# Token numbers spread by ScalarE and the first expert's rows turned on TensorE, in a two-layer mixture-of-experts kernel

## The reference

```python
y = einsum('bct,bcd->bdt', x, L0_cond_weights[itok])        # each block times a 128x128 matrix picked by index
probs = softmax(y.reshape(4096, 1024) @ gate_w.T)           # 64 experts
w, sel = top_k(probs, 8); w = w / w.sum(-1)
# each expert takes its first 256 tokens (capacity), in token order
h = silu(rows @ wg[e]) * (rows @ wu[e])                     # 256x1024 by 1024x384, twice
out = h @ wd[e]                                             # 256x384 by 384x1024
x = x + (sum over a token's experts of w * out)
```

## Time and profile before

| | |
|---|---|
| median of 3 runs | 2473.59 us (2473.21 to 2474.43) |
| profiled execution, its own time | 2452.17 us |
| its span | 2450.4 us |
| TensorE busy (of the span) | 2386.2 us, 97% |
| DVE / ACT / POOL busy | 70% / 52% / 58% |
| granted TensorE clock, mean | 0.989 |
| mean HBM traffic over the span | 239 GB/s |

### The profile page before, as it was taken

One profiled execution on the slowest core, in us unless ns is written; L12 is line 12 of the kernel. 1 busy time (PEld: TensorE's weight loads), 2 busy tenths in 40 slices (PEclk: granted clock), 3 DMA queues, 4 the chain that ended last, 5 costly groups with the idle time before them and its releaser, 6 DMA issues.

```text
span 2450.4 us, 35529 instructions
## 1 busy us (share of the span) xinstructions
PE 2386.2 (97%) x13055; PEld 2107.1 (86%) x13055; DVE 1718.6 (70%) x2993; ACT 1271.8 (52%) x1779; POOL 1422.6 (58%) x1044
## 2 busy tenths in 40 slices
PE   8977999999999999999999999999999999999998
PEld 6755888888888888888888888888879999999998
DVE  4666887878888787888878788887852255555553
ACT  4544666666666666666666666666651211111110
POOL 4017887777777777777777777777610122222221
PEclk9988999999999999999999999999999999999999
DMA  9977998888999889898998989898874444444441
GB/s 335 347 264 259 288 284 280 281 275 279 285 285 284 279 278 279 275 282 273 284 282 277 280 275 280 272 286 282 272 200 97 95 125 127 129 127 127 127 118 53
DMA packets 248799, 583.69 MB, mean 238 GB/s; under 512 B 82793, under 2 KB 105322, under 8 KB 248498
## 3 DMA queue, kind: packets, MB, share of 16 engines
q1 hardware_dynamic: 181426, 402.26, 49.7%
q0 software_dynamic: 55808, 160.28, 24.7%
q10 hardware_dynamic: 11392, 18.88, 2.1%
HBM read 460.97 MB, written 124.53 MB: 239 GB/s over the span
## 4 chain that ended last, share of the span: by engine, by line
PE 90%; DVE 2%; DMA 1%; ACT 0%; POOL 0%; issue 0%; DVEq 0%; POOLq 0%; ACTq 0%
PE ps L656 25%; PE ps L674 21%; PE ps L776 17%; PE ps L655 13%; PE ps L727 5%; PE ps L652 4%; PE ps L760 2%; PE ps L653 2%; PE ps L741 1%; POOL Xg L489 0%; PE ps L634 0%; DMA G<-tabd,rowi 0%; DVE g L1404 0%; DMA x<-in_L_ffn_base_w 0%; PE ps L749 0%
## 5 line engine op out<-in xcount | busy, mean ns | idle before, releaser
L656 PE MATMUL ps<-XX,HR 128*128 128x512 f32 x2688 | 959.2, 396 | 0.0
L489 POOL DMA_INDIRECT Xg<-yd,idx x512 | 694.9, 1357 | 162.8 <-issue 155.4
L655 PE MATMUL ps<-XX,LR 128*128 128x256 f32 x2688 | 750.1, 279 | 0.0
L1169 DVE TENSOR_TENSOR LR<-raw,HR 128x1536 fp32r<-128x1536 f32 x384 | 656.8, 1750 | 1.6 <-ACT HR L857 1.4
L656 PEld LDWEIGHTS ps<-XX,HR 128*128 128x128 f32 x2688 | 505.2, 188 | 104.2
L857 ACT ACTIVATE HR<-raw 128x1536 fp32r<-128x1536 f32 x384 | 555.1, 1477 | 3.3 <-DMA raw<-in_L_ffn_wd 1.8
L655 PEld LDWEIGHTS ps<-XX,LR 128*128 128x128 f32 x2688 | 507.5, 189 | 17.5
L511 POOL DMA_INDIRECT accd<-ot,toki x128 | 251.0, 1961 | 170.5 <-ACT ot L889 148.8
L674 PE MATMUL ps<-LR,hH 128*128 128x512 f32 x768 | 302.5, 394 | 0.0
L674 PE MATMUL ps<-HR,hL 128*128 128x512 f32 x768 | 301.0, 392 | 0.0
L674 PE MATMUL ps<-HR,hH 128*128 128x512 f32 x768 | 298.8, 389 | 1.4 <-DVE hL L1206 1.4
(11 more groups left out here) (171 smaller groups left out, 3487.3 us busy)
## 6 DMA issues: line engine op xcount, KB each, us to landing
raw<-in_L_ffn_wg SPq DMA_DIRECT2D x128, 768.0 KB, 8.0
raw<-in_L_ffn_wu SPq DMA_DIRECT2D x128, 768.0 KB, 6.8
raw<-in_L_ffn_wd SPq DMA_DIRECT2D x128, 768.0 KB, 4.5
xt<-in_x SPq DMA_DIRECT2D x32, 512.0 KB, 7.0
yd<-yrow ACTq DMA_DIRECT2D x32, 512.0 KB, 6.3
x<-accd SPq DMA_DIRECT2D x32, 512.0 KB, 4.7
out<-osb SPq DMA_DIRECT2D x32, 512.0 KB, 3.0
accd<-xt SPq DMA_DIRECT2D x24, 512.0 KB, 6.4
```

Source lines behind the costliest of these rows:

```text
L489: eng.indirect_dma_start(Xg[:, c, q, :], None, yd4, bass.IndirectOffsetOnAxis(ap=idx4[:, e % 4, i:i + 1], axis=0))\
L655: eng.matmul(bank(out, 0, CAP), wl, xx[:, 0:CAP], start=False, stop=False)
L656: mm = eng.matmul(bank(out), wh, xx, start=False, stop=(k == 7))
L1169: eng.tensor_tensor(LR[:, (n + 2) % NHL, :], raw[:, n % NRAW, :], HR[:, (n + 2) % NHL, :].bitcast(F32), ALU.subtract).then_inc(s_L, 1)
```

## The change

The eight-column spreading of the token numbers moves from DVE and TensorE to ACT: `tokq`, `qm`, `rep`, `repeat` and the semaphore `s_fl` go, `spread(e)` comes, and `index(e)` reads `tq` from SBUF. `spread` runs for experts 1 to 63. Expert 0 gets its rows by two indirect loads of whole 4 KB rows (`gather_rows`), TensorE turns them by 16 transposes into banks 4 to 7 (`turn_0`), ACT and DVE split them from there (`high_0`, `low_0`). The order of its channels is then another one, so the first four weight units are loaded in the matching order, by eight DMAs each. SP holds unit 4 and all behind it until both row gathers have landed. DVE takes `split("uB", 0)` before the second count, ACT issues a first Silu ahead of the rows. The semaphore values shift by one expert.

```diff
@@ SP, load_unit(n) @@
-                eng.dma_start(unit_dst(n), unit_src(n)).then_inc(d_raw[n % NRAW], 16)
+                if n < NRAW:
+                    k = units[n][0]
+                    v = (wg if k[0] == "g" else wu)[0].rearrange("(f a h j) i -> j h a f i", f=4, a=32, h=2)
+                    f0 = 0 if k[1] == "A" else 2
+                    d = raw[:, n, :].rearrange("p (f h i) -> p h f i", f=2, h=2)
+                    for j in range(4):
+                        for h in range(2):
+                            eng.dma_start(d[32 * j:32 * j + 32, h], v[j, h, :, f0:f0 + 2]).then_inc(d_raw[n], 16)
+                else:
+                    eng.dma_start(unit_dst(n), unit_src(n)).then_inc(d_raw[n % NRAW], 16)
...
+                if n == NRAW:
+                    eng.wait_ge(d_xg[0], 16)
+                    eng.wait_ge(d_xg[1], 16)
                 load_unit(n)
@@ POOL @@
-            eng.memset(rep[:, :], 0.0)
-            v = rep[:, :].rearrange("p (f t) -> p f t", f=4)
-            for q in range(4):
-                ch.link(eng.affine_select(out=v, in_=v, compare_op=ALU.not_equal, fill=1.0,
-                                          base=-32 * q, pattern=[[0, 4], [-1, 32]], channel_multiplier=1))
...
+            def gather_rows():
+                eng.wait_ge(d_wy, 16 * NB // 4)
+                for s in range(NY):
+                    eng.wait_ge(d_ys[s], 16 * len(range(s, NB, NY)))
+                for s in range(NS):
+                    eng.wait_ge(d_as[s], 16 * (NB // 4))
+                eng.wait_ge(s_tok, 2)
+                for c in range(2):
+                    eng.indirect_dma_start(Xg[:, c, :, :].rearrange("p q s -> p (q s)"), None, yd,
+                                           bass.IndirectOffsetOnAxis(ap=toki[:, c * E:c * E + 1], axis=0))\
+                       .then_inc(d_xg[c], 16)
...
             def gather_x(e):
+                eng.wait_ge(s_i4, e)
                 for c in range(2):
+                    if e >= 2:
+                        eng.wait_ge(s_vt, 2 * (e - 2) + c + 1)
+                    else:
+                        eng.wait_ge(s_x0, 2 * c + 2)
...
-            gather_x(0)
+            gather_rows()
@@ PE @@
-            def repeat(e):
...
-                eng.matmul(bank(4 + e % 2, 0, 8), rep[:, :], tokq[:, e % 4, :], start=True, stop=True)\
-                   .then_inc(s_f, 1)
+            def turn_0():
+                eng.wait_ge(s_cte, NB)
+                for c in range(2):
+                    v = Xg[:, c, :, :].rearrange("p q s -> p (q s)")
+                    eng.wait_ge(d_xg[c], 16)
+                    for k in range(8):
+                        mm = eng.transpose(bank(4 + 2 * c + k // 4, (k % 4) * P, (k % 4 + 1) * P), v[:, k * P:(k + 1) * P], ident[:, :])
+                        if k % 4 == 3:
+                            mm.then_inc(s_x0, 1)
...
-                        if g == 0 and b == 0 and 0 < e < E - 2:
-                            repeat(e + 2)
                     mm.then_inc(s_up, 1)
-                    if e == 0 and b == 1:
-                        repeat(2)
...
             def down(e):
-                eng.wait_ge(s_fl, min(e + 3, E))
...
-            repeat(0)
-            repeat(1)
+            turn_0()
@@ ACT @@
+            def spread(e):
+                eng.wait_ge(s_tok, 2 * e + 2)
+                if e >= 5:
+                    eng.wait_ge(s_i4, e - 4)
+                for q in range(4):
+                    eng.activation(tq[0:32, e % 4, q, :], tokf[32 * q:32 * q + 32, e % 4, :], ACT.Copy)\
+                       .then_inc(s_tq, 1)
+                eng.wait_ge(s_tq, 4 * e)
+                for f in range(1, 4):
+                    eng.activation(tq[32 * f:32 * f + 32, e % 4, :, :], tq[0:32, e % 4, :, :], ACT.Copy)\
+                       .then_inc(s_f, 1)
+
+            def high_0(n):
+                eng.wait_ge(s_x0, n + 1)
+                c, g = divmod(n, 2)
+                eng.activation(XX[:, 0, 4 * g:4 * g + 4, c * P:(c + 1) * P],
+                               bank(4 + n).rearrange("p (j t) -> p j t", j=4), ACT.Copy).then_inc(s_h0, 1)
...
             for k in ("gA", "uA", "gB", "uB"):
                 split(k, 0)
-            for c in range(2):
-                high_x(0, c)
+            eng.activation(sil[:, 0:1], pf[:, 0:1], ACT.Silu)
+            for n in range(4):
+                high_0(n)
+            spread(1)
             split("dA", 0)
             for e in range(E):
+                if 1 <= e < E - 2:
+                    spread(e + 2)
                 if e >= 1:
                     for o in range(4):
                         result(e - 1, o // 2, o % 2)
...
                 copy_2(3 * e + 1)
+                if e == 0:
+                    spread(2)
                 silu(3 * e + 1)
@@ DVE @@
-                eng.memset(qm[32 * q:32 * q + 32, q, :], 1.0)
...
+            def low_0(n):
+                eng.wait_ge(s_h0, n + 1)
+                c, g = divmod(n, 2)
+                lo, hi = CAP + c * P, c * P
+                mm = eng.tensor_tensor(XX[:, 0, 4 * g:4 * g + 4, lo:lo + P],
+                                       bank(4 + n).rearrange("p (j t) -> p j t", j=4),
+                                       XX[:, 0, 4 * g:4 * g + 4, hi:hi + P].bitcast(F32), ALU.subtract)
+                if g == 1:
+                    mm.then_inc(s_vl, 1)
...
             def index(e):
-                eng.wait_ge(s_f, e + 1)
-                eng.tensor_scalar(idx4[:, e % 4, :], bank(4 + e % 2, 0, 8), 4.0, f4[:, 0:1], ALU.mult, ALU.add)\
-                   .then_inc(s_i4, 1)
-                eng.wait_ge(s_i4, e + 1)
-                eng.engine_nop().then_inc(s_fl, 1)
+                eng.wait_ge(s_f, 3 * e)
+                eng.tensor_scalar(idx4[:, e % 4, :], tq[:, e % 4, :, :].rearrange("p q c -> p (q c)"), 4.0, f4[:, 0:1],
+                                  ALU.mult, ALU.add).then_inc(s_i4, 1)
...
             split("uA", 0)
             count(0)
             token(0)
-            index(0)
             split("gB", 0)
+            split("uB", 0)
             count(1)
             token(1)
+            for n in range(4):
+                low_0(n)
             index(1)
-            split("uB", 0)
-            for c in range(2):
-                turn_x(0, c)
-                low_x(0, c)
             split("dA", 0)
```

More of the change, by code:

```diff
@@ L93, in adaln_ffn_kernel @@
         f4 = sb("f4", [P, 1], F32)
-        rep = sb("rep", [P, P], F32)
-        qm = sb("qm", [P, 4, 2], F32)
         laR = sb("laR", [P, 8, NA, R], F32)
@@ L110, in adaln_ffn_kernel @@
         tokf = sb("tokf", [P, 4, 2], F32, moe)
-        tokq = sb("tokq", [P, 4, 8], F32, moe)
+        tq = sb("tq", [P, 4, 4, 2], F32, moe)
         idx4 = sb("idx4", [P, 4, 8], I32, moe)
@@ L221, in adaln_ffn_kernel @@
         s_H, s_L, s_up, s_dn = sem("s_H"), sem("s_L"), sem("s_up"), sem("s_dn")
-        s_f, s_fl, s_c2, s_gs = sem("s_f"), sem("s_fl"), sem("s_c2"), sem("s_gs")
+        s_tq, s_f, s_c2, s_gs = sem("s_tq"), sem("s_f"), sem("s_c2"), sem("s_gs")
         s_hh, s_hl = sem("s_hh"), sem("s_hl")
+        s_x0, s_h0 = sem("s_x0"), sem("s_h0")
         s_sl, s_hp, s_out, s_tok, s_wc = sem("s_sl"), sem("s_hp"), sem("s_out"), sem("s_tok"), sem("s_wc")
@@ L474, in gather_tab @@
                        .then_inc(d_g[e % 2], 16)
-            def gather_x(e):
-                eng.wait_ge(s_i4, e + 1)
-                if e == 0:
-                    eng.wait_ge(d_wy, 16 * NB // 4)
-                    for s in range(NY):
-                        eng.wait_ge(d_ys[s], 16 * len(range(s, NB, NY)))
-                    for s in range(NS):
-                        eng.wait_ge(d_as[s], 16 * (NB // 4))
+            def gather_rows():
[9 more added lines that the diff above has]
+                       .then_inc(d_xg[c], 16)
+            def gather_x(e):
+                eng.wait_ge(s_i4, e)
                 for c in range(2):
-                    if e:
-                        eng.wait_ge(s_vt, 2 * (e - 1) + c + 1)
+                    if e >= 2:
+                        eng.wait_ge(s_vt, 2 * (e - 2) + c + 1)
+                    else:
+                        eng.wait_ge(s_x0, 2 * c + 2)
                     for q in range(4):
@@ L853, in split @@
                 n = pos[(k, e)]
-                eng.wait_ge(d_raw[n % NRAW], 16 * (n // NRAW + 1))
+                eng.wait_ge(d_raw[n % NRAW], 16 * (n // NRAW + 8))
                 if n >= NHL:
@@ L857, in split @@
                 eng.activation(HR[:, (n + 2) % NHL, :], raw[:, n % NRAW, :], ACT.Copy).then_inc(s_H, 1)
+            def spread(e):
[14 more added lines that the diff above has]
+                               bank(4 + n).rearrange("p (j t) -> p j t", j=4), ACT.Copy).then_inc(s_h0, 1)
             def high_x(e, c):
-                eng.wait_ge(s_vt, 2 * e + c + 1)
+                eng.wait_ge(s_vt, 2 * (e - 1) + c + 1)
                 if e >= 2:
@@ L1052, in _ @@
             eng.memset(tacc[:, :, :], 0.0)
```

(15 more changed lines are left out.)

8 lines of the change are left out of this document (removed).

## The result

The changed kernel takes **2450.44 us** (median of 4 runs, 2445.88 to 2451.52), the kernel before 2473.84 (4 runs, 2473.21 to 2474.43): ratio 0.9902, 95% interval 0.9885 to 0.9919. That is 23.4 us less; forecast were 24.5 less, 2449.1 us and a range of 2445 to 2457. The time, the range and the direction hold. The terms behind them do not all hold: one is exact, two are wrong by several microseconds in opposite directions.

A forecast was written before the change was run, and what follows sets the result against it. TensorE, carrying 90% of the chain of waits, was taken to bound the kernel. Gains of 13.8 + 9.4 + 1.6 - 0.3 = 24.5 us, taken from the median 2473.59, gave 2449.1 us, range 2445 to 2457.

The forecast's parts named there:

- Term 1: Experts' steady stage: `repeat` leaves TensorE, the period falls from 25.247 to 25.02 us, 61 x 0.227 = 13.8 us gained.
- Rivals E and F: E: memory sets the pace, 2462.9 us, chance 0.04. F: `spread` late each time, only first stage gains, same time, 0.02.
- D: Steady stage: GpSimd becomes the pace, a period of 25.6 us, 2486 us in all; chance 0.03.
- (a): Before expert 0: with weight loads held, the second table gather lands at 176.1 instead of 179.2, 3.1 us gained.
- rival B: Table and row gathers stay as slow as before: up to 5.9 us less gain, about 2453 to 2455; chance 0.12.
- (b), (c): (b) Way to the first row gather 1.0 us shorter, issue at 177.7; (c) two gathers replace eight, landing at 184.2.
- (d): Expert 0's 16 transposes on TensorE: eight take 2.1 us at clock 1.00, 4.2 at 0.50; all done at 189.2.
- (e): Last quarter of expert 0's rows copied and subtracted; `up(0)` starts at 190.6 in place of 199.96, 9.4 us gained.
- (g): Expert 0's first `up` group: TensorE arrives awake after the transposes, so 1.6 us lost at half speed is won.
- rival A: Transposes leave the clock low: second eight at half speed (+2.1), 1.6 us not won, 2452.8 us; chance 0.17.
- Term 3: Rest of expert 0: the wait before L674 becomes about 3.2 us and silu runs 0.6 later; 0.3 us lost net.
- rival C: Held loads and fills meet the gather of expert 1's rows, lengthening the hL wait: 2449 to 2454 us; chance 0.13.

The follow-up runs named there:

- `pair_back`: The changed kernel with a matmul pair of the removed shape, result unused, and its wait put back into `up(e)`: 2447.65 us, ratio 0.9966.
- `no_hold`: The changed kernel without the hold, so unit 4 and those behind it load without waiting for both row gathers: 2440.09 us, ratio 0.9931.
- `wake`: The changed kernel with 30 matmuls, results unused, on TensorE ahead of the transposes of expert 0's rows: 2446.48 us, ratio 0.9885.
- `before_again`: The kernel before, unchanged, run again for a second profile: 2457.7 us.
- `after_again`: The changed kernel, unchanged, run again on another chip: 2434.04 us against 2456.19 for the kernel before, ratio 0.9908.
- `wake_turns`: The changed kernel with 36 transposes of the identity on TensorE ahead of the transposes of expert 0's rows: 2447.47 us, ratio 0.9902.
- `late_count`: The changed kernel with `count(3)` and `token(3)` on DVE moved behind the splits uA and gB of expert 1: 2432.53 us, ratio 0.99.
- `one_load`: The changed kernel with one DMA instead of eight for each of the first four weight units, matching channel order left out: 2434.16 us, ratio 0.9908.
- `fills_spread`: The changed kernel with FILL = 1, the `accd` fills issued one at a time instead of four at once: 2440.26 us, ratio 0.9933.
- the third group: Follow-up runs timed together on one chip, where the kernel before takes 2474.01 us.

## Why the prediction was right, and which steps were not

**Term 1, the pair: right.** 13.8 us forecast; the mean period went from 25.243 to 25.020, over the 61 periods from `down(1)` to `down(62)` 13.6, plus the call in `up(1)`, 0.2. `pair_back` shows that it is the pair. Rivals E and F (memory paces the stage, or the spread comes late) would have kept the period above 25.05 and D would have made it 25.6; none happened.

**What takes its place: right.** The seven copies last from 1017.59 to about 1019.17, 1.6 us for the 1.4 of the estimate, inside the idle of `high_x`.

**(a) The table gather: right.** 3.1 us forecast from a row of the second layer, 3.2 measured (6.20 to 3.00). `no_hold` shows it again at 6.64, so the price was the traffic beside it. That half of rival B is out; of its other half, the 2.8 us of a slow row gather, some 2 came.

**(b), (c) The row gathers: late and slow, inside their bounds.** The first issue came at 178.74 for 177.7, half of it because the way from the token cast's end to that issue fell from 1.3 to 0.8 us, where 1.0 was taken away. The last rows landed at 186.23 for 184.2. The first gather took 5.0 from the start of its issue, as forecast (5.2); it is the second that lands 5.48 behind its issue, not 3.8. Why is open: my 2.8 came from a gather of a quarter of the data, and the two big ones were in flight together, which the sum left out.

**(d) The transposes: mis-sized.** I read the row of L590, eight in 1.07 us, as four transposes in eight passes. It is eight transposes: eight of L646 also stand as x8 and take 1.06 us at 1.00 (`wake`) and 1.94 to 1.97 at 0.50. So (d) was about twice too dear at either level (the 2.1 for the second eight came near by chance, half the price at half the clock), and this paid for (b) and (c): `up(0)` began at 189.65, forecast 190.6.

**(e) The start of `up(0)`: right by luck, by errors that cancel,** and against `before_again`, which began 1.8 later than the profile of before, the gain is 12.1 instead of 9.4.

**(g) The clock: wrong.** I held that the transposes would wake TensorE. The stretches of `after_again` are at 0.50 until 195; `up(0)` ran cold for some 5.5 us and took 19.5. In "TensorE: Matmul & The Clock Gate", "Part 4: PE-mode transpose", the Trainium skill has transposes not count as activity; by that rule rival A gave the outcome, and A's outcome in this point did come. But its reason doesn't hold for these float32 transposes: in `wake_turns` 36 of them alone brought the clock to 1.00. What the case had were two bursts of 2 us with pauses around them. This step is worth 1.6 in the forecast and about nothing in the runs.

**Term 3, the rest of the first expert: mis-sized.** Forecast was a wait for hL of about 3.5 us; it measures 4.64 in `after_again`. From the second group's end to hL it took 15.7 us, for 14.2 in `before_again`. DVE's 0.67 and 0.43 of waiting for gathered rows had not been in my chain, and `spread(2)` held silu up by 0.8, not 0.6; `late_count` takes 1.4 of the wait away. (The terms given for this chain, 0.6 less 0.2 and 0.2, make a loss of 0.2, where the forecast wrote 0.3.) And I had costed the wait by its length only: the clock falls in it, which makes the 12 matmuls behind it 1.5 to 1.6 us longer. Forecast for expert 0 was 1.3 us shorter (0.3 lost, 1.6 by the clock); it is 3.5 longer. Of these 4.8 us, 2.6 lie in `down(0)` (4.7 longer, where 2.1 were forecast by its wait) and most of the rest in `up(0)`, 1.2 shorter where the wait for `repeat(2)` and the clock made 2.9. How long `up(0)` runs cold differs from trace to trace (`up(0)` takes 18.2 to 19.5 us in `after_again` and the variants of its kernel that ran beside a kernel before of 2456), so about a microsecond of this is chance.

**The edits costed at nothing: right.** `one_load` for the small loads. For the held loads the landings of dA and dB cost ScalarE 0.56 and 0.54 us of idle and nobody on the path. That the fills cost expert 0 anything (rival C) is not shown: DVE never waited for expert 1's rows in `after_again`, and the microsecond that `fills_spread` is shorter there lies in the clock.

**The sum** is right because 2.7 more at the start of `up(0)` stand against 4.8 less in the first expert: 24.5 + 2.7 - 4.8 = 22.4, beside 22.1 to 23.4 measured. That is luck: neither error was known, and nothing ties one to the other. Of the forecast's own signs of being wrong one came, the clock of 0.50 after 191, and the forecast time held all the same.

**The offset: it held between the medians, and was not understood when written.** The time was forecast as the median less 24.5, taking the 21.4 us between the profiled execution and the median as a constant. Where the kernel before takes 2474, all five traces of a changed kernel have a standstill of ScalarE of 6 to 8 us that ends at 32, four of them one of 3 to 4 us that ends between 20 and 22, and three one in expert 0; where it takes 2456, none of the eight traces has any. No trace of the kernel before with them exists, so that its runs of 2474 hold them is inferred, and their cause stays open. That the hold's bunch alone does not make them is shown by `after_again`.

## What to carry to other kernels

Look for what shares the memory with a transfer that somebody waits for: holding the weight loads and fills back until two gathers had landed was worth 8.5 us at the start of the first expert and 6.1 in the time, more than making the gathers fewer, but the fills had to follow at once, since spreading them out cost 6.2. Take a pair of tiny matmuls out of a full TensorE stream at the measured difference of two periods, not at its listed duration. Where a wait on TensorE is costed, add the slower matmuls behind it, since waits of 2.0 us and more made the 12 matmuls behind them 4.3 to 5.3 us long instead of 2.75, and one of 1.4 left them at 2.9.

## What was unexpected of the hardware

- A run of 36 transposes, 5.54 us, raised the granted clock from 0.50 to 1.00. Two runs of 1.95 us did not, and idles of 3.40 us, of 2.02, and of 1.91 and 1.57 around a burst of 1.1, let it fall again; 0.63 and 1.57 around such a burst did not.
- The rise of the clock came at different times behind the same work: `up(0)` began at 189.6 in two traces, after the same transposes, and the upper level came between 192 and 193 in one and between 195 and 196 in the other.
- The same gather of 128 x 1 KB landed in 2.5 to 3.0 us with the loads held and in 5.1 to 6.6 beside two weight loads; the pair of 512 KB gathers in 5.48 and 10.56 (time from the second issue).
- The same program takes 2456 us on two chips and 2474 in the first measurement and on the chip of the third group, where the changed kernels' traces have pauses of up to 4.1 and of 6.2 to 7.7 us in the router that the profile cannot give an owner.
